# A recurrence over 512 steps with an attention block ahead of it: filler matmuls in each step, and a new order of the heads

## The reference

```python
def step(carry, xw_t):
    a = xw_t + prev_h @ Wh            # 4 x 256 times 256 x 1024
    i, f, o = sigmoid(...); g = tanh(...)
    next_c = f * prev_c + i * g
    next_h = o * tanh(next_c)
```

## Time and profile before

| | us |
|---|---|
| median of 3 runs | 1965.04 (1926.76 to 1974.58) |
| the profiled execution, its own time | 1959.42 |
| its span | 1957.6 |
| PE busy | 1378.3 (70%) |
| DVE busy | 1170.0 (60%) |
| ACT busy | 914.1 (47%) |
| POOL busy | 553.8 (28%) |

### The profile page before, as it was taken

The page is one execution under the profiler, slowest core; times in us unless marked ns, Lnnn a source line. Parts: engine busy times, 40 slices in busy tenths (PEclk is TensorE's granted clock), DMA queues, the critical chain, the costliest instruction groups (busy, mean ns, idle before and its releaser), DMA issues.

```text
span 1957.6 us, 60062 instructions
## 1 busy us (share of the span) xinstructions
PE 1378.3 (70%) x22071; PEld 1183.1 (60%) x22071; DVE 1170.0 (60%) x6481; ACT 914.1 (47%) x3335; POOL 553.8 (28%) x1726
## 2 busy tenths in 40 slices
PE   3665666556787878787878787878776757675764
PEld 3544444345676767676767676767675656565653
DVE  5455555425676767666666666667655565656555
ACT  0333366535565545555555454545533343333333
POOL 4122222344333332323232323232324041313100
PEclk9767655565656555555555555555555555555555
DMA  7000000000000000000000000000000000000000
GB/s 215 0 0 0 0 1 1 1 1 5 3 8 2 8 2 8 2 8 2 8 2 8 2 8 2 8 2 8 2 8 2 7 7 2 5 2 5 2 5 4
DMA packets 16689, 18.00 MB, mean 9 GB/s; under 512 B 6036, under 2 KB 15384, under 8 KB 16408
## 3 DMA queue, kind: packets, MB, share of 16 engines
q1 hardware_dynamic: 13016, 10.51, 1.9%
q10 hardware_dynamic: 3392, 3.81, 0.7%
HBM read 12.21 MB, written 2.10 MB: 7 GB/s over the span
## 4 chain that ended last, share of the span: by engine, by line
PE 46%; DVE 13%; POOL 11%; issue 8%; ACT 8%; POOLq 1%; DVEq 0%; ACTq 0%
PE psum L687 18%; PE psum L663 7%; PE psum L626 6%; PE psum L634 5%; POOL sc L231 4%; PE psum L677 3%; DVE cnew L1140 3%; ACT ot L885 2%; DVE hl L1149 2%; PE psum L647 2%; DVE hl L1147 2%; PE psum L562 2%; DVE gO L1135 2%; ACT w L783 1%; ACT weights L787 1%
## 5 line engine op out<-in xcount | busy, mean ns | idle before, releaser
L687 PE MATMUL psum<-hl,wh 128*128 128x8 f16 x16384 | 525.9, 172 | 347.0 <-DVE hl L1149 346.4
L687 PEld LDWEIGHTS psum<-hl,wh 128*128 128x128 f16 x16384 | 505.9, 104 | 427.8 <-DVE hl L1149 408.0
L879 ACT ACTIVATE tA<-gA 128x16 f32<-128x16 f32 x512 | 110.4, 216 | 554.8 <-DVE gA L1131 552.9
L1131 DVE TENSOR_REDUCE gA<-psum 128x16 f32<-128x32 f32 x512 | 96.8, 189 | 281.4 <-PE psum L687 276.6
L279 POOL TENSOR_SCALAR sc<-sc 128x1 f32<-128x1 f32 x97 | 22.8, 235 | 766.7 <-DVE sc L1108 336.1
L1032 DVE TENSOR_TENSOR weights<-w,weights 128x256 f16<-128x256 f32 x512 | 208.2, 419 | 39.8 <-ACT weights L787 38.8
L231 POOL TENSOR_TENSOR sc<-sc,cst 128x1 f32<-128x1 f32 (+1 forms) x260 | 201.1, 773 | 48.1 <-POOL sc L279 18.1
L787 ACT ACTIVATE weights<-psum 128x512 f16<-128x512 f32 x256 | 149.6, 584 | 13.5 <-PE psum L574 13.5
L562 PE MATMUL psum<-qTs,kT 64*128 64x128 f16 x1024 | 151.1, 299 | 6.4 <-ACT weights L787 4.5
L783 ACT ACTIVATE w<-psum 128x512 f32<-128x512 f32 x256 | 149.8, 585 | 7.9 <-DVE weights L1032 5.5
L885 ACT ACTIVATE ot<-cnew 128x8 f32<-128x8 f32 x512 | 109.3, 214 | 81.9 <-DVE cnew L1140 32.0
(11 more groups left out here) (229 smaller groups left out, 2319.6 us busy)
## 6 DMA issues: line engine op xcount, KB each, us to landing
arena<-in_x_dram SPq DMA_DIRECT2D x4, 512.0 KB, 9.8
wf<-in_L_cond_w_f_dram SPq DMA_DIRECT2D x2, 1024.0 KB, 17.5
xr<-in_x_dram SPq DMA_DIRECT2D x64, 32.0 KB, 1.7
out_dram<-place SPq DMA_DIRECT2D x64, 32.0 KB, 1.6
qTs<-in_L_cond_w_ada_dram ACTq DMA_DIRECT2D x1, 1536.0 KB
oT<-in_L_cond_Wh_dram ACTq DMA_DIRECT2D x1, 1024.0 KB, 14.4
wx<-in_L_cond_Wx_dram SPq DMA_DIRECT2D x1, 1024.0 KB, 19.0
rows<-in_L_cond_b_ada_dram ACTq DMA_DIRECT2D x4, 128.0 KB, 14.8
```

The costliest lines, as they stand in the source:

```text
L687: last = mm(cols, wh16[:, half, kc, (g0 + c) * P:(g0 + c + 1) * P], hl[:, :, kc, :, 2].rearrange("p e b -> p b e"), start=False, stop=c == ...
```

## The change

- FIRST is -126. `head_slot` goes by block: block 0 one head per slot in slots -126 to -63, block 1 one head per step in steps 0 to 63, block 2 one in two steps from 64, block 3 one in two steps from 192. The last head stays at step 318. Slots -62 to -1 have no head.
- `weights` and `w32` are four deep, with the waits moved to match; the DVE reduction of eight heads (reciprocal and L1054) comes in one slot instead of two. In a slot ACT takes the second exponential of the last head first.
- `keep_busy(t)` at the end of each step 0 to 510 on PE: a wait for the reduction of gO of this step, then `count` matmuls of the f16 identity with a 128 x 256 tile of zeros, added into columns 256 to 511 of bank 6, which nothing else uses. `count` is 9 in a step with nothing else, less by weights for heads and pieces, 0 in the slots with L626, L663 and ahead of put_round.
- The waits for bank 3 go by an ordered list of its users, PM_ORDER: each waits for the reader of the one before.

```diff
--- before.py
+++ after.py
@@ -65,17 +65,20 @@
 NUMBERS = 800
 
 
-FIRST = -192
+FIRST = -126
 PAUSE = 48
 HEADS = B * NB * H
 RING = 32
 ROUND = 16
 LN2 = math.log(2.0)
+FILL = True
 
 
 def head_slot(n):
 
-    return FIRST + 2 * n
+    block = n // (B * H)
+    i = n % (B * H)
+    return (FIRST + i, i, 64 + 2 * i, 192 + 2 * i)[block]
 
 
 def merged_slot(k):
@@ -83,13 +86,22 @@
     return head_slot(H * k + H - 1) + 6
 
 
+HEAD_AT = {head_slot(n): n for n in range(HEADS)}
+PM_READ = {"merged": "m_oc", "rows": "n_n1", "norm": "n_nfc", "out": "o_s"}
+PM_ORDER = [use for slot, rank, use in sorted(
+    [(merged_slot(k) + 8, 0, ("merged", k)) for k in range(NT)] +
+    [(RING * n - PAUSE, 2, ("rows", n)) for n in range(NT)] +
+    [(RING * n - PAUSE + 30, 1, ("norm", n)) for n in range(NT)] +
+    [(RING * n + RING + 1, 3, ("out", n)) for n in range(NT)])]
+
+
 def pieces(g, attention, merged, post, out):
 
 
     attention(g)
-    k = (g - merged_slot(0)) // RING
-    if 0 <= k < NT:
-        merged(k, g - merged_slot(k))
+    for k in range(NT):
+        if 0 <= g - merged_slot(k) <= 8:
+            merged(k, g - merged_slot(k))
     newest = (g + PAUSE) // RING
     for n in (newest - 1, newest):
         if 0 <= n < NT and g + PAUSE - RING * n < PAUSE:
@@ -145,8 +157,9 @@
         xr = sb("xr", [P, 3, D])
         X = sb("X", [P, 3, D])
         hs = sb("hs", [P, 2, KD, B, RING])
-        weights = sb("weights", [P, 2, 2, T], F16)
-        w32 = sb("w32", [P, 2, T])
+        weights = sb("weights", [P, 4, 2, T], F16)
+        w32 = sb("w32", [P, 4, T])
+        zeros = sb("zeros", [P, D], F16)
         uo = sb("uo", [P, 2, D])
         osq = sb("osq", [P, D])
         oS = sb("oS", [P, D])
@@ -571,28 +584,29 @@
                     pe.wait_ge(s["t_u"], m // 8)
                 for kc in range(NB):
                     for wl in range(2):
-                        last = mm(pV[:, h % 8 * W1:(h % 8 + 1) * W1], weights[:, m % 2, wl, kc * P:(kc + 1) * P], vs[:, k % B, kc, h, :],
+                        last = mm(pV[:, h % 8 * W1:(h % 8 + 1) * W1], weights[:, m % 4, wl, kc * P:(kc + 1) * P], vs[:, k % B, kc, h, :],
                                   start=kc == 0 and wl == 0, stop=kc == NB - 1 and wl == 1, skip_group_check=True)
                 last.then_inc(s["t_AV"], 1)
 
             def attention(t):
 
-                if t % 2 == 1 and 0 <= (t - 5 - FIRST) // 2 < HEADS:
-                    weighted((t - 5 - FIRST) // 2)
-                if t % 2 == 0 and (t - FIRST) // 2 < HEADS:
-                    scores((t - FIRST) // 2)
+                if t - 5 in HEAD_AT:
+                    weighted(HEAD_AT[t - 5])
+                if t in HEAD_AT:
+                    scores(HEAD_AT[t])
+
+            def wait_pM(use, n):
+
+                before = PM_ORDER.index((use, n)) - 1
+                if before >= 0:
+                    kind, i = PM_ORDER[before]
+                    pe.wait_ge(s[PM_READ[kind]], i + 1)
 
             def merged(k, r):
 
                 if r == 8:
                     pe.wait_ge(s["m_oS"], k + 1)
-                    if k >= 6:
-                        pe.wait_ge(s["o_s"], k - 5)
-                    if k >= 4:
-                        pe.wait_ge(s["n_n1"], k - 3)
-                        pe.wait_ge(s["n_ga"], k - 3)
-                    if k >= 1:
-                        pe.wait_ge(s["m_oc"], k)
+                    wait_pM("merged", k)
                     for c in range(KD):
                         last = tr(pM[:, c * P:(c + 1) * P], oS[:, c * P:(c + 1) * P], ident[:])
                     last.then_inc(s["m_oT"], 1)
@@ -600,11 +614,8 @@
             def post(n, r):
 
                 if r == 0:
-                    pe.wait_ge(s["m_oc"], max(B * (n // B + 1), min(n + 4, NT)))
-                    if n >= 1:
-                        pe.wait_ge(s["n_nfc"], n)
-                    if n >= 3:
-                        pe.wait_ge(s["o_s"], n - 2)
+                    pe.wait_ge(s["m_oc"], B * (n // B + 1))
+                    wait_pM("rows", n)
...
@@ -637,12 +648,7 @@
...
-                        pe.wait_ge(s["m_oc"], min(n + 5, NT))
...
+                        wait_pM("norm", n)
@@ -700,19 +706,31 @@
             def out_rows(n):
 
                 pe.wait_ge(s["l_hs"], RING * (n + 1))
-                if n + 3 <= NT:
-                    pe.wait_ge(s["n_n1"], n + 3)
-                    pe.wait_ge(s["n_ga"], n + 3)
-                if n >= 1:
-                    pe.wait_ge(s["o_s"], n)
+                wait_pM("out", n)
                 for kc in range(KD):
                     last = tr(pM[:, kc * P:(kc + 1) * P], hs[:, n % 2, kc, :, :].rearrange("p b t -> p (b t)"), ident[:])
                 last.then_inc(s["o_T"], 1)
+
+            def keep_busy(t):
+
+                left = 1.0
+                left -= 0.35 * (t - 5 in HEAD_AT) + 0.25 * (t in HEAD_AT) + 0.3 * (t % RING == 1)
+                left -= 1.0 * ((t + 1) % ROUND == 0)
+                for r in ((t + PAUSE) % RING, (t + PAUSE) % RING + RING):
+                    if r < PAUSE and (t + PAUSE - r) // RING < NT:
+                        left -= 0.5 * (r == 0) + 0.3 * (r in (24, 41)) + 1.0 * (25 <= r < 29 or 42 <= r < 46) + 0.5 * (29 <= r < 33) + 0.4 * (r in (30, 31))
+                count = int(left / 0.11)
+                if count > 0:
+                    pe.wait_ge(s["l_gO"], t + 1)
+                    for i in range(count):
+                        mm(pO[:, D:2 * D], ident16[:], zeros[:], start=False, stop=False, skip_group_check=True)
 
             for t in range(FIRST, T):
                 if t >= 0:
                     step(t)
                 pieces(t, attention, merged, post, out_rows)
+                if FILL and 0 <= t < T - 1:
+                    keep_busy(t)
             out_rows(NT - 1)
 
         @block.scalar
@@ -774,17 +792,17 @@
 
             def attention(t):
 
-                m = (t - FIRST) // 2
-                if m < HEADS:
-                    if t % 2 == 0:
-                        act.wait_ge(s["t_S"], m + 1)
-                        if m >= 2:
-                            act.wait_ge(s["t_l"], 2 * m - 2)
-                        A(w32[:, m % 2, :], bank[m % 2], ACT.Exp, scale=1.0 / (math.sqrt(HD) * QK_UP * QK_UP)).then_inc(s["t_E"], 1)
-                    else:
-                        if m >= 2:
-                            act.wait_ge(s["t_AV"], m - 1)
-                        A(weights[:, m % 2, 0, :], bank[m % 2], ACT.Exp, scale=1.0 / (math.sqrt(HD) * QK_UP * QK_UP)).then_inc(s["t_e"], 1)
+                if t - 1 in HEAD_AT:
+                    m = HEAD_AT[t - 1]
+                    if m >= 4:
+                        act.wait_ge(s["t_AV"], m - 3)
+                    A(weights[:, m % 4, 0, :], bank[m % 2], ACT.Exp, scale=1.0 / (math.sqrt(HD) * QK_UP * QK_UP)).then_inc(s["t_e"], 1)
+                if t in HEAD_AT:
+                    m = HEAD_AT[t]
+                    act.wait_ge(s["t_S"], m + 1)
+                    if m >= 4:
+                        act.wait_ge(s["t_l"], 2 * m - 6)
+                    A(w32[:, m % 4, :], bank[m % 2], ACT.Exp, scale=1.0 / (math.sqrt(HD) * QK_UP * QK_UP)).then_inc(s["t_E"], 1)
 
             def merged(k, r):
 
...
+            d.memset(zeros[:], 0.0).then_inc(s["dinit"], 1)
...
@@ -1029,27 +1048,22 @@
 
                 part = slice(half * T // 2, (half + 1) * T // 2)
                 v.wait_ge(s["t_e"], m + 1)
-                d.tensor_tensor(weights[:, m % 2, 1, part], w32[:, m % 2, part], weights[:, m % 2, 0, part], ALU.subtract).then_inc(s["t_l"], 1)
+                d.tensor_tensor(weights[:, m % 4, 1, part], w32[:, m % 4, part], weights[:, m % 4, 0, part], ALU.subtract).then_inc(s["t_l"], 1)
 
             def attention(t):
 
-                m = (t - 2 - FIRST) // 2
-                if 0 <= m < HEADS:
-                    low_weights(m, t % 2)
-                m = (t - 5 - FIRST) // 2
-                if t % 2 == 1 and 0 <= m < HEADS and m % 8 == 7:
+                for half in (1, 0):
+                    if t - 2 - half in HEAD_AT:
+                        low_weights(HEAD_AT[t - 2 - half], half)
+                m = HEAD_AT.get(t - 5, 0)
+                if m % 8 == 7:
                     k, at_ = m // H, m % H // 8 * 8
                     v.wait_ge(s["t_AV"], m + 1)
                     if k >= 2:
                         v.wait_ge(s["m_F"], k - 1)
-                    d.reciprocal(num("rd", 2 * H)[:, k % 2 * H + at_:k % 2 * H + at_ + 8],
-                                 pV[:, 0:8 * W1].rearrange("p (h e) -> p h e", e=W1)[:, :, HD]).then_inc(s["t_rd"], 1)
-                m = (t - 6 - FIRST) // 2
-                if t % 2 == 0 and 0 <= m < HEADS and m % 8 == 7:
-                    k, at_ = m // H, m % H // 8 * 8
-                    if k >= 2:
                         v.wait_ge(s["m_sq"], k - 1)
                     two = pV[:, 0:8 * W1].rearrange("p (h e) -> p h e", e=W1)
```

(1 more changed line is left out.)

7 lines of the change are left out of this document (1 added, 6 removed).

## The result

The changed kernel takes **1977.44 us** (median of 20 runs, 1966.49 to 1993.31); the kernel before, 1962.88 (20 runs, 1926.76 to 1990.43). The ratio is **1.0171, 95% interval 1.0129 to 1.0212**. I had predicted 2040 us, 75 above the median then shown; the medians differ by 14.6 us, the profiled spans by 25.0, and the ratio makes it some 33. The direction was right, the size two to five times too large, and the time lies under the forecast's own range of 1990 to 2095.

A forecast was written before the change was run, and what follows sets the result against it. It took a plain step's 2.33 us loop through TensorE, VectorE and ScalarE as the bound, the clock counting only where TensorE's other work overflows. Terms -29 + 20 + 88 = +79 on 1959.4 gave about 2040 us; 8-in-10 range 1875 to 2100.

The forecast's parts named there:

- (1): Head stage ahead of step 0: fewer heads and deeper buffers shorten it, -29 us, bounds -10 and -45.
- (2): Steps 0 to 63: a head in each step adds VectorE, ScalarE and TensorE work, +20 us, bounds 0 and +45.
- (5): PSUM waits in the new order: 0 us, bounds -5 and +10 for a merge in GpSimd's mobius and norm pieces.
- (3): Fills from step 320: nine cost 0.88 us a step at 1.2 GHz, nothing at 2.4; 109 us if all low.
- (4): Clock in filled steps: mostly stays at 1.2 GHz, so fills cost +88 us, between 0 and 109.
- Rival A: Fills lift and hold the clock, cost nothing and shorten dense steps: 1870 us, from 1790 to 1935; chance 0.28.
- Rival B: Only the late part holds the high clock between full stretches; steps 64 to 319 stay low: 1950 us; chance 0.10.
- C: Fills are no load: nine cost far less than 1.92 us at the low clock: 1950 us; chance 0.05.

The follow-up runs named there:

- the two placings above: Changed kernel with old head slots and fills only in steps 320 to 463, ahead of the dense stretches or away from them: 1956.8 and 1956.38 us.

## Why the prediction was wrong

**(1) Head stage: -22.4 against -29.** Its main term was right. ScalarE's first exponential of head 63 starts at 331.54 us, 75.2 us after the first of all (256.34); I had said 75. The chain then reaches the output projection of tile 0, 20.5 us earlier than in the earlier trace rows (predicted 18), and from there to the first gate products it is 94.2 us against 96.2:

```profile
L693 PEld LDWEIGHTS psum<-hl,wh x16384: 95/103/291, 439.6 to 1976.5; 128*128 128x128 f16 x200
...
345.43 2.05 PE L620 MATMUL psum<-wo,oT 128*128 128x256 f32 x4 [0.56 <-ACT oT L819]
```

There I had taken 11 us off for heads that no longer stood in the way, and 2 came: they had hardly been on that chain.

**(2) Steps 0 to 63: +34.8 against +20.** Some eleven of it go with the clock: these steps had PEclk 0.59 in the kernel before, and with the old slots and no fills they take 180.5 us at 0.59 and 191.8 at 0.53 (the two placings above). The other 24 came in part from elsewhere than I wrote. Step by step against the 191.8, the kernel without fills takes 11 us more in steps 9 to 16 and 41 to 48, 6 in steps 25 to 29 and 57 to 61, and 7 in all others. The two VectorE halves, for which I had 16, thus cost little: most plain steps stay near 2.33 us, some take 2.6 to 2.7. The largest part stands in the full stretch, where every step now has scores and products ahead of its f32 pieces (changed kernel, TensorE, step 15):

```profile
486.36 1.00 PE L693 MATMUL psum<-hl,wh 128*128 128x8 f16 x32
487.22 0.39 PE L587 MATMUL psum<-vs,weights 128*128 128x33 f16 x8
487.54 0.60 PE L575 MATMUL psum<-qTs,kT 64*128 64x128 f16 x4
488.07 2.07 PE L645 MATMUL psum<-wf,arena 128*128 128x256 f32 x4
489.94 1.71 PE L653 MATMUL psum<-ones,arena 128*128 128x1 f32 x8
491.50 2.06 PE L683 MATMUL psum<-arena,ident 128*128 128x256 f32 x6
493.35 1.04 PE L693 MATMUL psum<-hl,wh 128*128 128x8 f16 x32
```

7.0 us from this step's products to the next ones, in the kernel without fills as well. Much of that is the 1.2 GHz clock: with the old slots the same step takes 6.3 us at 0.50 (at most five fills) and 3.8 at 1.00 (kernel before). And where a merge meets the norm of a tile, step 27 takes 6.5 us instead of 3.4 (timeline, POOL and DVE):

```profile
524.21 2.94 POOL L244 TENSOR_TENSOR sc<-sc,cst 128x16 f32<-128x16 f32 x1 [0.18 <-POOL sc L408]
...
532.85 0.15 DVE L1112 CAST sc<-sc 128x1 f32<-128x1 int32 x1 [4.03 <-POOL sc L260]
532.92 0.18 DVE L1145 TENSOR_REDUCE gA<-psum 128x16 f32<-128x32 f32 x1
```

GpSimd's power of the merge (2.94 us) stands ahead of the norm's operations; VectorE waits 4.03 us for the last of these, and the gate reduction is queued behind that wait. It comes twice; step 28 gives 0.6 us back each time, so it is some +5 us. It was in the bounds of (5), not in its value.

**(3) The fills' price** was right at both clocks, and so was the count. The tail answers to it: 38 steps of nine fills x 0.88 = 33.4 us; measured 33.3 for the whole tail against the kernel without fills.

**(4) Which clock: the step that failed.** It said that filled steps do not raise the clock, and that "the full stretches themselves get no fills and gain little". Set against the kernel without fills, by stage: in the tail predicted +34, measured +33.3; in steps 320 to 463 predicted 62 for 70 steps of nine, +3 for the sixes, less 21, so +44, **measured -2.9**; in steps 64 to 319 predicted about +18, less up to 9 absorbed, **measured -10.4**. Steps 0 to 63 changed by -0.5. In sum +88 against +20. Over all profiles, steps 320 to 463 take 401 to 418 us with nine fills (five kernels, mean 408) and 412 to 415 without (three): -5 rather than +44.

Steps 320 to 463, counted step by step by the starts of the gate products against the kernel without fills, show both halves of the error. The 70 steps of nine cost 34.9 us and not 62, for 42 of them took 3.20 us and the others less. The 54 steps without a fill, which the forecast had at nothing, took 33.1 us **less**. The rest gave 4.7. In steps 64 to 319 the 69 steps of six cost 21.2, and the 96 without a fill gave back 22.4. So the fills do act on the clock: what they lose in their own steps comes back in the unfilled ones behind them, above all in a full stretch, which takes 24.0 us at the high clock instead of 32.1. At most five fills do this almost free of cost (399.7 and 399.8 for steps 320 to 463, against 401 to 418 with nine). The sign that the prediction named for a wrong (4), a rise in steps 320 to 350 without a full stretch ahead of it, is in the trace: at 1491.5 us, behind filled steps and after 17 us at 1.2 GHz (from 1474.5). Without fills the clock is low there and rises only within or at the end of the full stretches. The sign of the total did not turn with it, because of the tail.

I had taken the clock's behaviour from f32 pieces and one rise, as two ends (0 or 109 us), and let the nearest row decide. That row was nearest in busy time, and busy time does not tell the two clocks apart here: TensorE is busy 92% of the tail with nine fills (135.37 of 147.7 us) at 0.51, and 91% of that with fourteen (119.67 of 131.6) at 0.98. The tail matches its +34: there the forecast was right. That the total came out on the forecast's side is no evidence for (4): it did so because the losses of the tail and of steps 0 to 63 were larger than gains that the forecast did not have.

Whether f32 pieces and f16 fills bear differently on the clock was not tried: no run replaces one by the other.

**Rival A** (1870) did not happen with nine fills, but eleven hold the clock at 2.4 GHz most of the time from step 320 on. It, too, had a price wrong: eleven stick out of the step (2.48 against 2.33 us), so they give 20 to 26 us in steps 320 to 463, where at most five fills give 12.5, and cost 4 in the tail. **Rival B** (1950) comes near in time only without the tail's fills (1954.17), and not by its own account: steps 64 to 319 gained as well, and its sum takes 20 for the five tiles whose product is 35. **C** is refuted by the 3.21 us between filled steps.

## What to carry to other kernels

Fill first only the time that is idle even at the low clock: at most five fills cost 1.4 us over 84 steps and brought 12.5 us in steps 320 to 463. Beyond that the gain is not steady in the amount. Nine cost their full price at the low clock (408 us on average, little under none at all), eleven held the clock in most of the stage (386 to 393), fourteen gave it all back (416); so try a step more and a step less before judging the idea. Put fills only where work that the clock speeds up follows: in the tail, where nothing gained by the clock is on the path, the same fills could only lose. And where identical code differs by 24 us between runs because of the clock, judge variants by stage, with the granted clock beside each, not by the total of one run; a stage, too, differed by up to 18 us in one profile each of the same code.

## What the runs showed of the hardware

- More matmuls made a stage faster. The tail took 147.7 us with nine fills a step at 1.2 GHz; with eleven 118.5, twelve 123.1 and fourteen 131.6 it ran at 2.4 GHz (PEclk 0.94 to 0.98). None and at most five, at 1.2 GHz: 114.3 and 116.1.
- The data of the fills made no difference to the clock in the tail: zeros by an identity and weights by weights gave 147.7 us and PEclk 0.51 alike.
- A few matmuls in the gaps of a step changed the clock of the dense stretch behind them: with at most five, the four full stretches read above took 25.8 to 30.7 us (PEclk 0.83 to 0.61) instead of 29.9 to 32.1 (0.61 to 0.55).
- The time at the high clock in the same instructions differed by run: 936.7 to 961.0 us for steps 0 to 319 in five profiles of one program, 940.9 and 964.5 in two of another. The Trainium skill, TensorE: Matmul & The Clock Gate, section "The HAM clock gate", has the number of matmuls at the low clock vary from run to run, and puts the penalty of the rise at under 1% of a typical span. Here, where the clock rises and falls many times, the difference between two runs is 1.2% of the span.
